# P times V of two heads packed into eleven full rounds, in four batches instead of six

## What is computed

```python
qkv = (h @ Wqkv.T + bqkv).reshape(B, N, num_heads, hd, 3)      # layer 0: B 4, N 1024, 16 heads, hd 32
energy = jnp.einsum('bhqd,bhkd->bhqk', q, k)
att = jax.nn.softmax(energy, axis=-1) / D ** 0.5
out = jnp.einsum('bhqk,bhkd->bhqd', att, v)
...
attn = jax.nn.softmax(jnp.einsum('bhqd,bhkd->bhqk', q, k) * hd ** (-0.5), axis=-1)   # layer 1, the same sizes
o = jnp.einsum('bhqk,bhkd->bhqd', attn, v).transpose(0, 2, 1, 3).reshape(B, T, D)
```

## Time and profile before

| | us |
|---|---|
| three timed runs | 3014.92, 3023.49, 3024.56 |
| median | 3023.49 |
| the profiled execution | 3021.92 |
| its span, first to last instruction | 3020.1 |

### The profile page before, as it was taken

The page is one execution under the profiler, slowest core; times in us unless marked ns, Lnnn a source line. Parts: engine busy times, 40 slices in busy tenths (PEclk is TensorE's granted clock), DMA queues, the critical chain, the costliest instruction groups (busy, mean ns, idle before and its releaser), DMA issues. The chain is left out here.

```text
span 3020.1 us, 70269 instructions
## 1 busy us (share of the span) xinstructions
PE 2781.6 (92%) x22313; PEld 1481.0 (49%) x22313; DVE 2246.9 (74%) x4482; ACT 1839.4 (61%) x3287; POOL 1987.6 (66%) x1677
## 2 busy tenths in 40 slices
PE   7899999999999989999569998998999899958998
PEld 6654466444755547454235444544444445524444
DVE  4777688776877778777667768776877787738997
ACT  3366655665556654666346676667666766657887
POOL 0288824886268841889438885887788688854441
PEclk9999999999999999999889999999999999979999
DMA  6122343223422324222133213322232222143000
GB/s 210 43 54 53 125 133 100 54 69 120 154 70 58 116 105 131 63 53 74 40 108 81 55 23 107 80 58 53 79 75 58 64 73 61 39 152 134 31 28 35
DMA packets 101853, 243.28 MB, mean 81 GB/s; under 512 B 18620, under 2 KB 24900, under 8 KB 100552
## 3 DMA queue, kind: packets, MB, share of 16 engines
q1 hardware_dynamic: 99784, 233.49, 27.1%
q0 software_dynamic: 1792, 6.33, 0.6%
HBM read 99.15 MB, written 38.88 MB: 46 GB/s over the span
## 5 line engine op out<-in xcount | busy, mean ns | idle before, releaser
L459 DVE TENSOR_REDUCE b_mxs<-ps 128x1 f32<-128x512 f32 x1024 | 636.2, 684 | 198.4 <-PE ps L340 197.3
L459 DVE TENSOR_REDUCE a_mxs<-ps 128x1 f32<-128x512 f32 x1024 | 635.4, 683 | 176.7 <-PE ps L340 175.5
L425 ACT ACTIVATE a_p<-ps 128x512 f32<-128x512 f32 x1024 | 530.4, 602 | 242.3 <-PE ps L354 237.1
L425 ACT ACTIVATE b_p<-ps 128x512 f32<-128x512 f32 x1024 | 533.5, 602 | 201.3 <-PE ps L354 196.2
L312 POOL TENSOR_TENSOR b_sum<-b_p 128x512 f32<-128x512 f32 x384 | 496.7, 1297 | 87.2 <-ACT b_p L425 86.8
L312 POOL TENSOR_TENSOR a_sum<-a_p 128x512 f32<-128x512 f32 x384 | 498.2, 1301 | 68.6 <-ACT a_p L425 68.3
L340 PE MATMUL ps<-b_k,b_q 96*128 96x512 f32 x1024 | 443.6, 438 | 33.7 <-DVE b_mxs L459 23.3
L340 PE MATMUL ps<-a_k,a_q 96*128 96x512 f32 x1024 | 417.9, 417 | 6.8 <-DVE a_mxs L459 3.7
L354 PE MATMUL ps<-b_q,b_k 98*128 98x512 f32 x1024 | 400.1, 425 | 11.0 <-ACT b_p L425 7.8
L354 PE MATMUL ps<-a_q,a_k 98*128 98x512 f32 x1024 | 396.2, 421 | 9.8 <-ACT a_p L425 9.8
L368 PE MATMUL ps<-a_p,a_vx 128*32 128x512 f32 x2048 | 372.1, 599 | 10.7 <-POOL a_sum L317 8.9
(11 more groups left out here) (267 smaller groups left out, 4157.3 us busy)
## 6 DMA issues: line engine op xcount, KB each, us to landing
a_q<-a_qh SPq DMA_DIRECT2D x128, 128.0 KB, 2.3
a_k<-a_kh SPq DMA_DIRECT2D x128, 128.0 KB, 2.3
b_q<-b_qh SPq DMA_DIRECT2D x128, 128.0 KB, 2.3
b_k<-b_kh SPq DMA_DIRECT2D x128, 128.0 KB, 2.4
a_p<-in_w_fc SPq DMA_DIRECT2D x12, 1024.0 KB, 8.5
a_kl<-in_x SPq DMA_DIRECT2D x4, 2048.0 KB, 8.4
a_q<-a_ql SPq DMA_DIRECT2D x64, 128.0 KB, 2.3
a_k<-a_kl SPq DMA_DIRECT2D x64, 128.0 KB, 2.3
```

The source lines that it names most:

```text
L425: act.activation(self.key_tile(u, kt), self.st[RING[CHUNKS * (k % NJ) + n]], ACT.Exp, scale=self.scale).then_inc(self.s_exp, 1)
L459: dve.reduce_max(self.mxs[:, c:c + 1], self.mx[RING[CHUNKS * j + c]], axis=AX.X).then_inc(self.s_mxr, 1)
```

## The change

P times V is planned for two heads together, an even and an odd one: their 4 halves have 32 key tiles and 12 sums, 44 matmuls, in 11 full rounds. Where a half ends within a round, the free column groups take tiles of the next half, so rounds 2, 5 and 8 hold matmuls of two halves, which go to banks 6 and 7; round 8 has two sums. For half 1 the sums sit in column group 0 instead of 3, hence a second `fold` matrix. The batches are now after s = 2 and s = 6 of each head: odd head s = 2: `out_transpose` 0, rounds 3, 4, 5; odd s = 6: `out_transpose` 1, rounds 6, 7; even s = 2: rounds 8, 9, 10 of the pair before, then `out_transpose` 0; even s = 6: `out_transpose` 1, rounds 0, 1, 2. So the segments hold 8 pairs each. `out_copy` goes to s = 3 and (for half 0 of an even head) s = 7, `m_parts` to s = 2, `m_transpose` and `m_row` to s = 4, `divide` of half 0 to s = 2 (odd) or 3 (even) behind the step's first reduction, of half 1 to s = 6. There are five sum buffers, each with a fixed list of users; two `mxs` sets instead of one, two `mrow` tiles instead of four. `dq_t` shares the space of `mod_t`, with a wait that it needs. The last pass of a sequence has 7 steps.

```diff
-    ROUNDS = 3
-    PV_CREDIT = 4 * ROUNDS
-    SET = NJ + 1 + 1 + ROUNDS + 1
+    SUM = TT
+    VALUES = (((0, 0), (0, 1), (0, 2), (0, SUM)), ((0, 3), (0, 4), (0, 5), (0, SUM)), ((0, 6), (0, 7), (1, 0), (0, SUM)),
+              ((1, SUM), (1, 1), (1, 2), (1, 3)), ((1, SUM), (1, 4), (1, 5), (1, 6)), ((1, SUM), (2, 0), (2, 1), (1, 7)),
+              ((2, 2), (2, 3), (2, 4), (2, SUM)), ((2, 5), (2, 6), (2, 7), (2, SUM)), ((3, SUM), (3, 0), (3, 1), (2, SUM)),
+              ((3, SUM), (3, 2), (3, 3), (3, 4)), ((3, SUM), (3, 5), (3, 6), (3, 7)))
+    ROUNDS = len(VALUES)
+    PER_HALF = 3
+    SUM_USED = (0, 1, 2, 3, 4, 5, 6, 7, 8, 8, 9, 10)
+    SUM_AT = (0, 1, 2, 0, 4, 2, 3, 0, 1, 2, 3, 4)
+    SUM_PRIOR = (7, 8, 9, 0, 11, 2, 10, 3, 1, 5, 6, 4)
+    LAST = (2, 5, 8, 10)
+    FREED = (0, 0, 0, 1, 1, 1, 2, 2, 3, 3, 3, 4, 4, 4, 5, 5,
+             6, 6, 6, 7, 7, 7, 8, 8, 8, 8, 9, 9, 9, 10, 10, 10)
+    PV_CREDIT = ROUNDS
+    SET = NJ + 1 + 1 + 2 * (3 + 1)
     NP = STEPS
-    NS = 4
+    NS = 5
...
+    def sums(self, pool, N, M, j):
+
+        u, r = j // self.PER_HALF % 2, j % self.PER_HALF
+        tile, kt = self.sum[:, self.SUM_AT[j], :], 3 * r
+        prior = self.SUM_PRIOR[j]
+        pool.wait_ge(self.s_pv, self.ROUNDS * (M - (prior > j)) + self.SUM_USED[prior] + 1 + self.PV_CREDIT)
+        pool.wait_ge(self.s_exp, CHUNKS * N + TT * u + kt + 1 + 1 + self.EXP_CREDIT)
+        pair = pool.tensor_tensor(tile, self.key_tile(u, kt), self.key_tile(u, kt + 1), ALU.add)
...
+    def values_round(self, pe, E, r):
+
+        new = [half for half, _ in self.VALUES[r] if all(half != other for n in range(r) for other, _ in self.VALUES[n])]
+        for half in sorted(set(new)):
+            pe.wait_ge(self.s_o, 2 * E + half + 1)
+            if half % 2 == 0:
+                pe.wait_ge(self.s_vx, E + half // 2 + 1)
+        used = [j for j, n in enumerate(self.SUM_USED) if n == r]
+        pe.wait_ge(self.s_exp, CHUNKS * E + max(TT * half + kt for half, kt in self.VALUES[r] if kt != self.SUM) + 1 + self.EXP_CREDIT)
+        pe.wait_ge(self.s_sum, 2 * self.PER_HALF * E + used[-1] + 1)
+        for c, (half, kt) in enumerate(self.VALUES[r]):
+            rounds = [n for n in range(self.ROUNDS) if self.VALUES[n][c][0] == half]
+            at = [j for j in used if j // self.PER_HALF == half]
+            tile, weights = ((self.sum[:, self.SUM_AT[at[0]], :], self.ones[:, :]) if kt == self.SUM else
+                             (self.key_tile(half % 2, kt), self.vx[half // 2][:, kt, :]))
+            mm = pe.matmul(self.ot[half % 2][HD * c:HD * (c + 1), :], weights, tile, start=r == rounds[0], stop=r == rounds[-1])
+        mm.then_inc(self.s_pv, 1)
...
-                after_values = s in (0, 2, 5)
+                after_values = s in (3, 7)
...
-                if s == 1 and ok(k - 1):
-                    self.out_transpose(pe, 2 * N - 2, 0)
-                    self.values_round(pe, k - 1, N - 1, 1, 1)
-                    self.values_round(pe, k - 1, N - 1, 1, 2)
-                if s == 3 and ok(k + 1):
-                    pe.wait_ge(self.s_o, 2 * N + 1)
-                    self.m_transpose(pe, N + 1, 0)
-                if s == 4 and ok(k - 1):
-                    self.out_transpose(pe, 2 * N - 1, 1)
-                if s == 4 and ok(k):
+                if s == 2 and ok(k - 1):
+                    if k % 2:
+                        self.out_transpose(pe, 2 * N - 2, 0)
+                        for r in (3, 4, 5):
+                            self.values_round(pe, N - 1, r)
+                    else:
+                        for r in (8, 9, 10):
+                            self.values_round(pe, N - 2, r)
+                        self.out_transpose(pe, 2 * N - 2, 0)
+                if s == 4 and ok(k + 1):
+                    pe.wait_ge(self.s_ots, 2 * N + 1)
+                    self.m_transpose(pe, N + 1, 1)
+                if s == 6:
                     if ok(k + 1):
                         pe.wait_ge(self.s_mrow, N + 2)
-                    self.values_round(pe, k, N, 0, 0)
-                    self.values_round(pe, k, N, 0, 1)
-                if s == 7 and ok(k):
-                    self.values_round(pe, k, N, 0, 2)
-                    self.values_round(pe, k, N, 1, 0)
+                    if ok(k - 1):
+                        self.out_transpose(pe, 2 * N - 1, 1)
+                    if ok(k):
+                        for r in (6, 7) if k % 2 else (0, 1, 2):
+                            self.values_round(pe, N - k % 2, r)
...
-                if s in (0, 2) and ok(k - 1):
-                    self.out_copy(act, 2 * N - 2 + s // 2, s // 2)
+                if s == 3 and ok(k - 1):
+                    for u in (1,) if k % 2 else (0, 1):
+                        self.out_copy(act, 2 * N - 2 + u, self.pair(b, i, k - 1), (k - 1) % 2, u)
+                if s == 7 and ok(k) and k % 2 == 0:
+                    self.out_copy(act, 2 * N, self.pair(b, i, k), 0, 0)
...
-                if ok(k + a):
-                    for c in range(2):
+                for c in range(2):
+                    if ok(k + a):
                         self.reduce_chunk(dve, N + a, (k + a) % NJ, (2 * s + c + CHUNKS - 4) % CHUNKS)
-                if s == 1 and ok(k + 1):
-                    self.m_parts(dve, N + 1)
-                if s in (1, 4) and ok(k - 1):
-                    self.divide(dve, 2 * N - 2 + s // 4, s // 4, 4 * i + k - 1)
+                    if s == (2 if k % 2 else 3) and c == 0 and ok(k - 1):
+                        self.divide(dve, 2 * N - 2, 0, 4 * i + k - 1)
+                    if s == 6 and c == 0 and ok(k - 1):
+                        self.divide(dve, 2 * N - 1, 1, 4 * i + k - 1)
+                if s == 2 and ok(k + 1):
+                    self.m_parts(dve, N + 1, (k + 1) % NJ)
```

More of the change, by code:

```diff
@@ L209, in setup_pool @@
         fill(self.ones[:, :], 1.0)
[L211 to L216, removed]
+        fill(self.fold[:, :, :], 0.0)
+        for u, sums in enumerate((3 * HD, 0)):
+            for r in range(0, P, HD):
+                if r != sums:
+                    ch.mark(pool.affine_select(out=self.fold[:, u, 0:HD], in_=self.fold[:, u, 0:HD], compare_op=ALU.not_equal,
+                                               fill=1.0, base=-r, pattern=[[-1, HD]], channel_multiplier=1))
+                    ch.wait()
+            fill(self.fold[sums:sums + 1, u, HD:HD + 1], 1.0)
         assert ch.n == self.SET
@@ L239, in call @@
             ok = (lambda kk: 0 <= 4 * i + kk < H) if known else (lambda kk: True)
-            head(i, k, H * b + n, ok, 5 if known and n == H else STEPS)
+            head(i, k, H * b + n, ok, 7 if known and n == H else STEPS)
         if flat:
@@ L250, in loop, with pair @@
             call(NQ - 1, k, True)
+    def pair(self, b, i, k):
+        return H // 2 * b + 2 * i + k // 2
     def load(self, sp, b, N, row, j):
@@ L302, in key_tile @@
         return self.p[:, 4 * u + kt // 2, kt % 2 * HALF:(kt % 2 + 1) * HALF]
[L304 to L319, removed]
+    def sums(self, pool, N, M, j):
[5 more added lines that the diff above has]
+        pair = pool.tensor_tensor(tile, self.key_tile(u, kt), self.key_tile(u, kt + 1), ALU.add)
+        if kt + 2 < TT:
+            pair.then_inc(self.s_part, 1)
+            pool.wait_ge(self.s_part, 2 * (2 * N + u) + r + 1)
+            pool.wait_ge(self.s_exp, CHUNKS * N + TT * u + kt + 2 + 1 + self.EXP_CREDIT)
+            pool.tensor_tensor(tile, tile, self.key_tile(u, kt + 2), ALU.add).then_inc(self.s_sum, 1)
+        else:
+            pair.then_inc(self.s_sum, 1)
@@ L321, in run_pool @@
     def run_pool(self, pool, b, flat=False):
-        self.value(pool, 0, H * b, 0)
+        self.value(pool, 0, H * b, self.pair(b, 0, 0), 0)
         def head(i, k, N, ok, steps):
             if ok(k):
-                self.sums(pool, k, N, 0)
+                for n in range(self.PER_HALF):
+                    self.sums(pool, N, self.pair(b, i, k), 2 * self.PER_HALF * (k % 2) + n)
             if ok(k + 1):
-                self.value(pool, 4 * i + k + 1, N + 1, (k + 1) % 2)
+                self.value(pool, 4 * i + k + 1, N + 1, self.pair(b, i, k + 1), (k + 1) % 2)
@@ L329, in head @@
             if ok(k):
-                self.sums(pool, k, N, 1)
+                for n in range(self.PER_HALF, 2 * self.PER_HALF):
+                    self.sums(pool, N, self.pair(b, i, k), 2 * self.PER_HALF * (k % 2) + n)
         self.loop(pool, b, head, flat)
@@ L355, in scores @@
                   self.q[j][0:98, u * HALF:(u + 1) * HALF], start=True, stop=True).then_inc(self.s_st, 1)
[L357 to L368, removed]
-                          start=r == 0, stop=kt + 3 >= TT)
-        pe.matmul(self.ot[u][3 * HD:4 * HD, :], self.ones[:, :], self.sum[:, at % self.NS, :],
-                  start=r == 0, stop=r == self.ROUNDS - 1).then_inc(self.s_pv, 1)
+    def values_round(self, pe, E, r):
[14 more added lines that the diff above has]
+        mm.then_inc(self.s_pv, 1)
```

(7 more changed lines are left out.)

45 lines of the change are left out of this document (22 added, 23 removed).

## The result

The changed kernel takes 2975.57 us (median of 4 runs, 2973.25 to 2976.52), the kernel before beside it 3022.65 (3014.92 to 3024.56): a ratio of 0.9848, 95% interval 0.983 to 0.9866. The forecast was 2974.5 in a range of 2940 to 3012. The profiled execution is one of 2976.52 us with a span of 2974.7.

A forecast was written before the change was run, and what follows sets the result against it. PE's time was taken to bound the attention. Eight sequences x (5.8 + 1.1) give 55 us less, last heads 5 more, POOL set-ups 1 more: 49 less, so 2974.5 us against the median 3023.49, range 2940 to 3012.

The forecast's parts named there:

- Batches: P times V batches on PE: 11.25 us in two heads instead of 12.32, a gain of 1.07.
- Segments: PE's stretches of 8 pairs between batches: four take 17.4 us in two heads, against 16.90 before.
- the last term of the chain: In the sum for a segment's eighth chunk, which needs reduction 5: 0.33 us from last chunk to batch.
- the signs that I had set down: Prediction wrong if a round waits for a sum, mixed half-rounds are further apart, segments exceed 4.6, or heads' clock is below 1.00.
- The ring's 0.95 in four heads: Short bank distances in long segments: eighth chunk needs reduction 6, fourth score the second's exponential (0.45); 0.95 us in four heads.
- The better case of 2916: Whole kernel: two heads at 27.5 us by PE alone, DVE's divide and rings costing nothing; 2916 to 2960 had chance 0.1.
- POOL: POOL's sums within heads: 27.2 us of work fits into 28.6; it waits for round 0 but stops nobody.
- The ends: Ends of a sequence: head 0 gains 1.1 us; last two heads 1.7 more in layer 0, 0.5 less in layer 1.
- Rival 3: PE's clock falls as it waits more often: 4 us at 1.2 GHz in two heads gives 3102 us; chance 0.02.
- The row of the maximum: Later max parts and `m_row` transfer in a segment: no cost, unless the DMA took over 4 us.
- Rival 1: Long batches starve DVE and ACT: 0.5 us more in two heads, 3003; 2985 to 3014 chance 0.2, same 0.07, worse 0.02.
- Rival 2: Mixed rounds 2, 5 and 8 run in turn, half-rounds double: 2.6 us in two heads, 3141 us; chance 0.04.

The follow-up runs named there:

- The first run: The changed kernel with P times V unpacked again: each half has its own three rounds, twelve in four batches; 3032.06 us, 1.0043 of the kernel before.
- The run with the row first: Changed kernel with later divide, turned maximum ring and reordered sum buffers, plus head 14's maximum row transferred before layer 0's four late loads; 2962.88 us.

## Why the prediction was right

**Batches.** Right, and shown to be the cause. 11.23 for 11.25 in two heads. The first run puts the round back and loses it all, of which the round itself is 5.7 of the 7.9 us in heads 1 to 13.

**Segments.** The sum of 17.4 is right for one kind of pair, and 17.67 for the other: 17.5 in the mean, and terms of it were a little too small. The divide's segment takes 4.64 where I had 4.5. I took the divide at 0.45 to 0.52, and between the two reductions around it DVE's queue loses 604.72 - 604.18, 0.54: this is the smaller part. The larger is the last term of the chain, 0.33 from the last chunk to the batch: a chunk that has waited stands 0.43 ahead of the batch.
```profile
607.25 0.49 PE L359 MATMUL ps<-a_k,a_q 96*128 96x512 f32 x1
...
607.68 0.46 PE L398 MATMUL ps<-a_fold,a_ots 128*32 128x33 f32 x32
```
So by one of the signs that I had set down, segments over 4.6, the working was wrong here: 4.64, and 4.78 to 4.80 for the segment with the maximum's short distances, which I had at 4.6. The ring's 0.95 in four heads is measured as 0.68 for the maximum (both its short distances fall into one segment; I had counted one) and 0.34 for the score. The plain segments are 4.10 as forecast, in every experiment; those with only an `m_transpose` are 4.14 to 4.22. That these three places were limits of their own, and not shadows of each other, is shown by the runs that remove them one at a time: 2.89 (divide), 1.71 (ring of the maximum) and 0.98 (ring of the scores) in heads 1 to 13. What is left, 180.12, is 27.7 for two heads; my figure for PE alone was 27.5. The better case of 2916 supposed that divide and rings cost nothing; it took these further edits (and the sum buffers) to come there, 2918.

That heads 1 to 13 nevertheless came out at 5.8 less, as forecast, is in part luck. In a pair the divide and the short distances all stand in the even head's half, which takes 15.1 or 15.5 us, the odd head's 13.5; and heads 1 to 13 are six even and seven odd ones. I had counted 6.5 pairs. With my own terms the odd half is 4.1 + 3.03 + 4.15 + 2.16 = 13.44, and six pairs with one odd half more are 6 x 28.62 + 13.44 = 185.2; the window is 185.91, 0.7 more, some 6 us in eight sequences. The two errors nearly cancel.

**POOL.** Once in two heads it waits, for round 0, as worked out, and stops nobody within the heads (186.10 without the wait). At the end it counts, by 0.85 us in the one sequence read and by 4 to 7 us in all.

**The ends.** Head 0 was 1.1 less in the forecast. The whole attention of one sequence of layer 0 is 5.54 less, for 5.2 forecast: 5.8 in heads 1 to 13, about 1 in head 0, and 1.2 given back in the last two heads, for 1.7. One wait there was not foreseen: in head 14's steps the divide of head 13's half 1 stands behind DVE's work for the next sequence (`spare`), and round 2 waits for it.
```profile
695.82 0.63 PE L391 MATMUL ps<-a_p,a_vx 128*32 128x512 f32 x3 [0.91 <-DVE a_tok L505]
...
712.15 0.59 PE L391 MATMUL ps<-a_sum,a_unit 128*32 128x512 f32 x1 [1.48 <-POOL a_sum L334]
...
714.72 0.59 PE L391 MATMUL ps<-a_sum,a_unit 128*32 128x512 f32 x1 [1.51 <-POOL a_sum L334]
```
The other two rows are the POOL end that I did foresee. In the first sequence of layer 1 the stretch from head 14 to the end went from 38.01 (1776.81 to 1814.82) to 38.5, 0.5 more for 0.5 less forecast: PE's waits for POOL moved to its end. Since all ends together are some 5 us, it doesn't show.

**Layer by layer.** From the end of one sequence's attention to the next, the three of layer 0 that follow the first took 4.78, 2.64 and 3.22 us less (358.88, 358.57 and 358.18 before); I had 5.2 for each. The stage between them, with the same work, has 119.82 for 119.06 us, at a granted clock of 0.97 for 0.99. I had put nothing there. The 2.64 and the 3.22 also pay for a granted clock at half around the end that they share; Rival 3, below, takes it up. Two such stretches of layer 1 took 7.18 and 10.19 less, for 7.4. The errors have both signs: the profiled execution came out at 2976.5 for 2973.

**The row of the maximum.** Put at no cost as long as its transfer took under 4 us. This holds in the heads: no wait for it in the window. At head 14 of layer 0 the condition is broken, as SyncE has issued loads of 2048, 2048, 1024, 512 and 256 KB ahead of it (5.9 MB, not the 4 that my expectations say). The changed kernel is late enough by then not to feel it; most of the faster ones did (0.37 to 1.11 us in the sequence read).

**Rival 1.** DVE idles 1.73, 1.73, 1.23 and 0.94 us ahead of its first reduction after the four batches, up to 0.7 more than my 1; and no hand-over but the foreseen ones is late. The 0.5 us in two heads didn't come.

**Rival 2.** No: half-rounds of a shared round are 0.43 apart, and the run with twelve unshared rounds has the slower window.

**Rival 3.** Not within the heads: 1.00 in all windows of them. But it did happen at ends of sequences, and I had missed it. PE at the end of the third sequence of layer 0:
```profile
1066.55 0.59 PE L391 MATMUL ps<-a_sum,a_unit 128*32 128x512 f32 x1 [1.47 <-POOL a_sum L334]
...
1069.12 1.03 PE L391 MATMUL ps<-a_sum,a_unit 128*32 128x512 f32 x1 [1.51 <-POOL a_sum L334]
...
1069.94 1.06 PE L391 MATMUL ps<-a_sum,a_unit 128*32 128x512 f32 x1
...
1074.76 5.43 PE L926 MATMUL ps<-ident,a_tok 128*128 128x128 f32 x32 [0.63 <-DVE a_tok L505]
```
Half-rounds are 0.82 to 0.86 apart and the granted clock is 0.50 in the windows from 1069 to 1077.5; the same steps of the sequence before have half-rounds 0.43 apart, 3.71 us for the 32 transposes, and a clock of 1.00. The stretch from 1066.55 to the transposes is 8.21 us instead of 6.68, and that from their start to the next product 6.27 instead of 4.54, 3.3 us in all, of which 1.5 belong to the 2.64 above and 1.7 to the 3.22. The kernel before has 1.00 at all four ends of layer 0. The waits for POOL ahead of it are the same in both sequences (1.47 and 1.51, 1.48 and 1.51), so they alone don't decide it, and what does stays open. The run with the row first shows the price after a long wait: after 10.0 us in which PE did nothing, the granted clock is 0.50, the lower level of 1.2 GHz, and half-rounds are 702.14 - 701.29 = 0.85 apart instead of 0.43. The Trainium skill, "TensorE: Matmul & The Clock Gate", section "What's actually happening", gives an idle PE half the clock of a busy one; this trace agrees. With the many short waits that PE has in the heads, 0.2 us each, it stays at 1.00.

## What to carry to other kernels

When each unit of work leaves a part of a fixed-width round empty, let neighbours share the round, and price it by the round that disappears, not by fewer switches: here 0.87 us in two heads, and four batches with the round unshared were slower than six (12 us, in part by late starts that no run explains). Look then at which engine the longer stretches couple: short work of DVE in front of a chain of reductions, and a ring whose count doesn't divide the loop, cost 20 us each where the change gained 47, and both could be moved to a place where they cost next to nothing. Count a sequence by the kinds of units in it: thirteen heads were not 6.5 average pairs. A wait on an in-order queue has everything behind it: before a load is moved later, find who waits for it, and what stands behind that wait.

## What the runs showed of the hardware

Column groups of one round may write two PSUM banks at once, three groups one half's and one the other's (rounds 2 and 8) or two and two (round 5), at the full rate: 0.43 us for a half-round of 512 columns, as when all four write one bank. PE's granted clock fell to 0.50 after an idle stretch of 10.0 us and is 0.99 in the window that begins 5.3 us after work resumed (701.29 to 706.60), a cost of 6 x 0.42 = 2.5 us on top of the wait. So long a wait is not needed. In the same run half-rounds are 0.84 apart once more from 717.26 on, with no such idle stretch ahead of them; with the divide later the clock is 0.51 behind a wait of 1.11 us; and in the changed kernel it is 0.50 behind waits of 1.47 and 1.51 us, which in the sequence before left it at 1.00. What decides it no run here shows.
